# Plain attention on one core: the sums of a half move one slot back in TensorE's order, and the copies of finished sums move behind the next two exponentials

## The reference

```
qkv = einsum('bnd,ed->bne', layernorm(x), W_qkv)      # 16 heads of 8
scores = einsum('bhnd,bhmd->bhnm', q, kk) / sqrt(8)
A = softmax(scores, axis=-1)
out = einsum('bhnm,bhmd->bhnd', A, v)                 # x = x + out
```

## Time and profile before

| what | us |
|---|---|
| median of 3 runs | 1890.01 |
| lowest and highest of them | 1889.61, 1891.53 |
| the profiled execution, its own time | 1893.23 |
| its span in the profile | 1891.5 |
| what lies around the span | 1.7 |

### The profile page before, as it was taken

The page is one execution under the profiler, slowest core; times in us unless marked ns, Lnnn a source line. Parts: engine busy times, 40 slices in busy tenths (PEclk is TensorE's granted clock), DMA queues, the critical chain, the costliest instruction groups (busy, mean ns, idle before and its releaser), DMA issues. The chain is left out here.

```text
span 1891.5 us, 33776 instructions
## 1 busy us (share of the span) xinstructions
PE 1643.9 (87%) x12964; PEld 630.1 (33%) x12964; DVE 1192.6 (63%) x2130; ACT 1442.4 (76%) x2508; POOL 314.4 (17%) x420
## 2 busy tenths in 40 slices
PE   5799999999999999864888888989889888883995
PEld 3222222222222222251333333433343333222674
DVE  7999989999999999886454536354545423223220
ACT  4478777777777777724999999999989999992221
POOL 4500010010011010032000100010001032312466
PEclk9899999999999999977999999999999999996997
DMA  5311111111111110004111211123111222231433
GB/s 169 99 38 38 38 44 38 38 44 38 38 38 44 39 40 19 12 21 151 45 43 55 85 58 51 53 68 98 51 47 63 86 82 93 96 118 59 124 57 30
DMA packets 70960, 115.86 MB, mean 61 GB/s; under 512 B 10041, under 2 KB 55973, under 8 KB 66192
## 3 DMA queue, kind: packets, MB, share of 16 engines
q1 hardware_dynamic: 59536, 92.88, 15.5%
q0 software_dynamic: 11264, 20.83, 4.0%
HBM read 71.49 MB, written 42.14 MB: 60 GB/s over the span
## 5 line engine op out<-in xcount | busy, mean ns | idle before, releaser
L786 ACT ACTIVATE rows_and_probs<-psS 128x512 f32<-128x512 f32 x1010 | 549.1, 596 | 166.7 <-PE psS L684 165.9
L808 DVE TENSOR_REDUCE max_of_halves<-psM 128x2 f32<-128x1024 f32 x512 | 623.6, 1224 | 54.6 <-PE psM L647 20.3
L1647 ACT ACTIVATE exps<-cpsS 128x1024 bf16<-128x1024 f32 x512 | 546.3, 1109 | 25.4 <-PE cpsS L1389 24.8
L1389 PE MATMUL cpsS<-rotary_stack 128*128 128x512 bf16 x1024 | 301.8, 384 | 72.4 <-ACT exps L1647 30.7
L704 PE MATMUL psO<-rows_and_probs,plain_v 128*9 128x256 f32 x4096 | 317.7, 382 | 5.3 <-ACT rows_and_probs L786 0.6
L1657 ACT ACTIVATE cprobs<-cpsS 128x1024 f32<-128x1024 f32 x256 | 281.7, 1100 | 21.6 <-PE cpsO L1422 18.9
L1369 PE MATMUL cpsS<-rotary_stack 128*128 128x512 bf16 (+3 forms) x768 | 193.6, 329 | 53.6 <-ACT exps L1647 36.5
L647 PE MATMUL psM<-plain_top 64*128 64x512 bf16 x1024 | 205.8, 384 | 20.9 <-DVE max_of_halves L808 20.5
L684 PE MATMUL psS<-plain_top 64*128 64x512 bf16 x1010 | 208.4, 388 | 0.0
L684 PE MATMUL psS<-plain_rest 64*128 64x512 bf16 x1010 | 202.6, 378 | 0.0
L1422 PE MATMUL cpsO<-cprobs,rotary_v 128*9 128x512 f32 (+3 forms) x1536 | 153.7, 488 | 0.8 <-DVE rotary_sums L1981 0.8
(11 more groups left out here) (301 smaller groups left out, 1758.2 us busy)
## 6 DMA issues: line engine op xcount, KB each, us to landing
rotary_stack<-q_parts SPq DMA_DIRECT2D x48, 192.0 KB
rotary_stack<-k_parts SPq DMA_DIRECT2D x48, 192.0 KB
rotary_stack<-q_rot_parts SPq DMA_DIRECT2D x48, 192.0 KB
rotary_stack<-k_rot_parts SPq DMA_DIRECT2D x48, 192.0 KB
tokens_taken<-parts_and_sums POOLq DMA_DIRECT2D x32, 259.0 KB, 4.1
plain_top<-q_parts SPq DMA_DIRECT2D x64, 96.0 KB
plain_top<-k_parts SPq DMA_DIRECT2D x64, 96.0 KB
e_x<-tokens_taken SPq DMA_DIRECT2D x8, 518.0 KB, 9.8
```

Source lines behind the costliest of these rows:

```text
L786: act.activation(pr[n % SLOTS_P][:, h, :], score_bank(u), ACT.Exp, scale=SCALE).then_inc(s_e, 1)
L808: dve.tensor_reduce(mh[g % 2][cq][:, :, hh, t, kh:kh + 1].rearrange("p e o -> p (e o)"), psM[n % 2][:, :, :], AX.X, ALU.max).then_inc(s_r, 1)
L1389: ins = pe.matmul(to[:, kh, :], q[:, x, y_ * P:(y_ + 1) * P], k[:, x, kh * CH:(kh + 1) * CH], start=True, stop=True)
L1647: act.activation(ex[d % EX][:, :, :], psS[n % 3][:, :, :], ACT.Exp, scale=SCALE, accum_out=den[:, at:at + 1]).then_inc(s_e, 1)
```

## The change

It moves instructions of two engines and adds none: `earlier` now runs in slot 0 part 1 of the half two back, and in slot 1 part 0 of the half before. The two copies by `keep` move from behind the fourth exponential of half 0 (or half 8) to behind the second exponential of half 1 (or half 9). Behind the last slot, part 1 of half 14 is added ahead of the two parts of half 15.

```diff
-            def earlier(g, half, part):
-                if half:
-                    av(g, half - 1, part)
-                elif g:
-                    av(g - 1, HALVES - 1, part)
+            def earlier(g, half, slot):
+
+                n, part = (g * HALVES + half - 1, 0) if slot else (g * HALVES + half - 2, 1)
+                if n >= 0:
+                    av(n // HALVES, n % HALVES, part)
...
             for g in range(G):
                 exp_group(g)
+            av(G - 1, HALVES - 2, 1)
             for part in range(2):
                 av(G - 1, HALVES - 1, part)
...
-                        if half == 0 and i == HG - 1 and g:
+                        if half == 1 and i == 1 and g:
                             keep(g - 1, 1)
-                        if half == TB and i == HG - 1:
+                        if half == TB + 1 and i == 1:
```

## The result

| what | before | changed |
|---|---|---|
| median of 19 runs each, us | 1890.72 | 1895.12 |
| lowest and highest, us | 1888.93, 1894.18 | 1892.02, 1898.16 |
| the profiled execution, its time and span, us | 1893.23, 1891.5 | 1894.13, 1892.4 |
| ratio | | 1.002, interval 1.0013 to 1.0027 |

What follows compares the result with a forecast made beforehand. TensorE's own order was taken to set the time (busy 41.45 of 42 us). Only the copies cost, 30 x 0.11 = +3.3 us on a median of 1890.0, giving 1893.3, other terms 0; range 1888.8 to 1897.0.

Steps and rivals of the forecast that it cites:

- Steady halves, term 0: Plain attention, sums one slot later: part 0's wait for exponentials costs nothing now, so removing it gives 0.
- Rival F: Part 0's wait makes a half 2.65, not 2.60; removal gives 0.05 in about 180 halves, so 1884.3; chance 0.09.
- The copy, +0.11: Pair of slots with a copy takes 2.88 (2.92 after a half 0), not 2.77 (2.81): 0.11 us more each.
- The two parts of it, 0.06 and 0.05: Copy follows exponentials starting at 0.70, not 0.64 (0.06); its wait no longer hides the late second score (0.05).
- The 0.08 in hand: Behind the copy, ACT's first exponential frees the bank at 2.80, before the next half's second score needs it at 2.88.
- rival S: Exponentials delayed behind the copy hold up the next half too; with 0.1 more a copy +6.3, 1896.3; chance 0.18.
- The last group, 0: Halves 10 to 15 save 0.9 us on TensorE, but DVE's chain sets the end: term 0, -0.9 at best.
- The count of copies: 31 copies for which the sums wait: 17 rows name the copy as releaser, 14 POOL's value fill; 30 counted.
- The sum: Whole kernel: +3.3 us, 1896.5 for the profiled execution, 1893.3 for a median; chance 0.55 for +2.4 to +4.2.
- N: Copy and its reader keep their distance and hide the same 0.05; term 0, 1889.1 to 1890.0; chance 0.18.

Runs made afterwards that it cites:

- the wait moved: Kernel before and changed kernel, each with ACT's wait on the sums of four halves ago put ahead of the previous half's fourth exponential: 0.9968 and 0.9977.

## Why the prediction was right

**Steady halves, term 0.** Right. Halves without a copy stay at 2.65, with the late score in slot 1. Rival F is out in both its parts: the changed order removed a wait that wasn't late, and the 0.05 went away when the semaphore was dealt with, in either order of the sums.

**The copy, +0.11.** Right to a hundredth: 1.67, 2.33 and 2.88 were forecast and are in the rows; behind a half 0 the forecast was 2.92, from 2.81, where the starts give 2.93 (755.15 to 758.08), from 2.82 (753.07 to 755.89). The two parts of it, 0.06 and 0.05, were only argued in the prediction. They are shown by the two kernels with the wait moved, which are alike although one has the change and the other hasn't.

**The 0.08 in hand (rival S).** It held: the slot behind the copy is 1.30.

**The last group, 0.** Right: TensorE is early by 1.5, DVE takes the merge behind its own chain.

**The count of copies.** The 31 is right, but not by the working of 17 rows and 14. The 17 are 16 weight loads and one matmul, all behind the 16 copies that follow half 8 of a group. The 14 are copies behind a half 0; the fifteenth of these, with the sums at 754.03, is put down to no engine. 16 and 15 make the 31.

**The sum.** +3.3 forecast, 3.2 by the turns, 3.8 (2.5 to 5.1) by the runs. 1893.3 was forecast from a median of 1890.0; over 19 runs the kernel before has 1890.7 and the changed one 1895.1, within the range. The 0.6 between turns and runs is inside the interval and not explained. The chances were set with the forecast just under 0.2%, and it came out on that line. The lower end of the range, 1888.8, isn't N less a microsecond, which is 1888.1; nothing hangs on it here.

**A size that was a little off.** The 0.05 of all steady halves was priced with 12 of 16 halves in 15 groups, 9 us (the size of F, not its cause). With the wait moved a group took 0.36 less, and each of its two pairs of slots with a copy 0.04 to 0.05 more (2.87 for 2.82 behind a half 0), so the other halves gave 0.45 a group, 6.7 us. The prediction left out that the merge, too, stretches slot 0 of its half and hides the late score there, so eleven halves had one and not twelve. One of the eleven, half 5, gave nothing: what its last slot became shorter, the next one, behind the turn, waited longer for DVE (0.02 to 0.03). The other ten gave 0.04 to 0.05 each.

## What to carry to other kernels

Where two engines hand tiles to each other in a ring, read the distances from start to start and in every slot of the period, since a difference of 0.05 between two like slots names the hand-over that binds. Of several waits ahead of one instruction, write the one that is satisfied last ahead of the others, or put those long satisfied where the engine has work queued; here this was tried on ACT alone. And before moving an operation behind another, ask what the wait that it causes was hiding.

## What the runs showed of the hardware

- The order of two waits on one ACT instruction matters by 0.06 us: 0.70 from the scores to the exponential with the late semaphore waited for last, 0.63 to 0.64 with it first, or alone. How the two waits are served isn't shown by a profile.
- A single dip of the granted clock, 3.4 us at 0.50 (0.93 over 25 us), cost 1.53 us between two turns. Six such dips lie in five of the nine profiles, all right behind the same waits of TensorE for DVE (about 1.0 and 0.4 us), which in 21 other places were followed by none, and a profile that has one more or less would be taken for a loss or gain of a change of 0.2%.
- In this ring of three banks a late start doesn't add up: with the exponentials of every slot 0.06 late, an ordinary half took 2.65, as long as with those of every second slot late.
- ACT copied 128 x 512 float32 out of PSUM in 0.60 us and 128 x 256 in 0.39 to 0.40, so half a copy takes about two thirds of the time of a whole one.
